# A decoder kernel on one core: the widest projection built anew with fp16 halves, its stores not waited for at its end, and one layer's queries and keys kept in SBUF

## The chip, the cores and the metric

The kernel runs on one core of a Trainium2 chip. The metric is the device time of one execution in microseconds (us). Three executions of the kernel before gave a median of 3291.48 us. The core's engines are TensorE (PE in the profile; PEld is its weight load), VectorE (DVE), ScalarE (ACT), GpSimd (POOL) and SyncE (SP), which here only issues DMAs. Each runs its own instructions in order and waits for others by semaphores.

## The reference

A decoder of four layers on x (2 x 1024 tokens of 256 numbers) and a context. Each layer is self-attention, cross-attention and a feed-forward part, each with a residual and a normalisation. Three places matter here.

Layer 0's feed-forward part sends each token to 4 of 32 experts; its end is

```
y = sum over the 4 chosen experts j of weight[t, j] * expert_out[slot[t, j]]
x = layernorm(x + y + shared)
```

Layer 1's self-attention has 16 query heads and 4 key/value heads of 64 numbers with a rotary embedding:

```
q = x @ Wq (256 -> 1024);  k = x @ Wk (256 -> 256);  v = x @ Wv (256 -> 256)
rope(a): (a1, a2) -> (a1 * cos - a2 * sin, a1 * sin + a2 * cos)
o = causal softmax(rope(q) rope(k)^T / 8) v;   x = layernorm(x + o @ Wo (1024 -> 256))
```

Layer 2's self-attention has one head of 256 numbers:

```
q, k, v = x @ Wq, x @ Wk, x @ Wv (256 -> 256 each);  o = causal softmax(q k^T / 16) v
```

## The kernel before, in words

The stages run one after another; a `Phase` holds a stage's tiles and semaphores and ends with a barrier of all engines. x lies twice in SBUF: by rows in `k.xr`, by columns in `k.xtr` (both in the tile `res`). The 2048 tokens are 16 tiles of 128, four groups (NG) of 512, two batches (B) of 1024.

**l1p**, the stage that the change rewrites, is `project_in` with `ahead=combine`. POOL gathers the four experts' rows of each tile by indirect DMA (line 2529, 64 gathers into 12 slots `yg`); VectorE adds them, weighted, onto `acc` (line 2538), adds the residual, takes the statistics (2551) and normalises (2564). TensorE turns the rows of a group into columns (2581), ScalarE copies them to `k.xtr` (2573). After two groups the projection begins, in fp32: ten jobs of 128 columns of W and 1024 tokens in each batch (line 1811, tile `res` against `l1p_w`), in pairs, "first" and "second" half of four heads, and two jobs of values. For a pair VectorE multiplies both halves by cos and sin out of PSUM into `tmp` (1886, 1887), POOL subtracts and adds into `st` (1914, 1915), ScalarE writes the fp16 upper part `his` (1830), VectorE the lower part `los = st - his` (1863), and SP stores the pair with 16 DMAs (1786) into `l_q_h`, `l_q_l`, `l_k_h`, `l_k_l` in DRAM. The additions for the third and fourth group stand between the pairs of batch 0. ScalarE doesn't write `his` before all 16 stores of the pair before have landed:

```
1829  after(act, ph.s["rstored"], 16 * 2 * job.n_dst * r)
1830  act.activation(his[:, half, :], st[:, half, :], ACT.Copy).then_inc(ph.s["hi_done"], 1)
```

At its end SP waits for all stores (1795). In batch 1 SP also loads the attention's first slot (`FirstSlot.queries`, `keys`), after batch 0's stores; POOL has filled constant rows of it (`fill`, two MEMSETs).

**l1a** is `packed_attention`. SP loads q and k of a pair of steps into a slot (`load`, lines 877 and 880), the second and third slot at the stage's start, and then moves the rows' maxima of each step (`maximum_rows`, 892). TensorE computes the maxima's products (1011) two steps ahead, then the scores (1042); the pass is shared by all engines. **l1o** is `project_columns`: o_t (1024 x 2048, fp32) against Wo in fp32 (line 1308, 8 matmuls of 256 columns a tile), then `Tail`, residual and normalisation of each group.

**l2p** is `project_in` again, in fp32, with jobs of kind "store": ScalarE copies to `st`, SP stores to DRAM (1771). **l2a** (`attention`) begins with two loads of these tensors (428, 429) and then makes its scores (460).

## Time and profile before

| | us |
|---|---|
| three executions | 3291.48, 3284.66, 3299.39 |
| the profiled execution | 3290.18 |
| its span in the profile | 3288.4 |
| PE busy | 2498.7 (76%) |
| DVE busy | 1872.2 (57%) |
| ACT busy | 1441.7 (44%) |
| POOL busy | 978.9 (30%) |

A busy share is a mean over stages that differ. The times below are counted from the start of the span. In a row of the timeline "x32" says that 32 instructions are merged, and the bracket gives the idle time before them and what ended it. An fp32 matmul leaves two records in the trace. The granted clock is a share of 2.4 GHz, and it has two levels, 1.2 and 2.4 GHz.

### The profile page before, as it was taken

Reading aid. Unit: us, or ns where it says so; the run is one execution under the profiler, and the core shown is the slowest. Engines: PE = TensorE matmul, PEld = TensorE weight load, DVE = VectorE, ACT = ScalarE, POOL = GpSimd, SP = SyncE. Lnnn points to the kernel's source line nnn. Section 1 sums busy time; section 2 is a strip of 40 time slices with the busy share of each in tenths; the row PEclk is TensorE's granted clock in tenths of the full one; section 3 lists DMA queues with packets and bytes.
Section 4 is the critical chain, followed back from the end, with each engine's and each line's share of the span. In section 5 each row is a group of like instructions: output and inputs, shape, how many; then the busy total and the mean of one; then the engine's idle time right before and its main releaser. Section 6 shows DMA issues by size and latency. Waiting matters only on the chain. (4 is left out here: it accounts for less than half of the span.)

```text
span 3288.4 us, 44258 instructions
## 1 busy us (share of the span) xinstructions
PE 2498.7 (76%) x15490; PEld 1395.0 (42%) x15490; DVE 1872.2 (57%) x5013; ACT 1441.7 (44%) x2899; POOL 978.9 (30%) x802
## 2 busy tenths in 40 slices
PE   6788885785725688888884679887776788859987
PEld 2223334564522333333362255555443333346666
DVE  6566655465748555555423558235442577656677
ACT  5334451454411256666611524214411355537876
POOL 1245561145355366666602400001101101101200
PEclk9889997897967889999986879998688799978988
DMA  3311101710555311111002210111000322114023
GB/s 111 99 36 42 42 2 36 233 50 17 156 147 90 92 54 36 45 40 36 17 14 66 34 39 1 61 52 34 14 0 27 78 28 28 16 47 122 1 78 103
DMA packets 185741, 182.87 MB, mean 56 GB/s; under 512 B 55161, under 2 KB 152187, under 8 KB 184751
## 3 DMA queue, kind: packets, MB, share of 16 engines
q1 hardware_dynamic: 176110, 167.48, 18.2%
q0 software_dynamic: 9408, 12.56, 2.6%
q8 instruction: 124, 2.03, 0.3%
q14 instruction: 99, 0.80, 0.1%
HBM read 121.81 MB, written 61.59 MB: 56 GB/s over the span
## 5 line engine op out<-in xcount | busy, mean ns | idle before, releaser
L941 POOL TENSOR_TENSOR l1a_p_lo<-res,l1a_p_hi 128x1024 f16<-128x1024 f32 x192 | 311.6, 1641 | 178.5 <-ACT res L1182 178.5
L1191 ACT ACTIVATE l0a_probs<-ps 128x1024 f32<-128x1024 f32 (+1 forms) x192 | 145.7, 810 | 178.1 <-PE ps L1045 105.7
L1191 ACT ACTIVATE l3a_probs<-ps 128x1024 f32<-128x1024 f32 (+1 forms) x192 | 146.7, 809 | 142.4 <-PE ps L1045 115.2
L1181 ACT ACTIVATE l1a_p_hi<-ps 128x1024 f16<-128x1024 f32 x192 | 157.8, 822 | 112.3 <-PE ps L1045 83.0
L1042 PE MATMUL ps<-l1a_qs,l1a_ks 128*128 128x512 f16 (+3 forms) x768 | 167.4, 332 | 32.2 <-ACT res L1182 32.2
L1213 DVE CUSTOM_DVE_ANT_0 l1a_masked<-ps,l1a_wide_mask 128x128 bf16<-128x128 f32 (+3 forms) x256 | 118.1, 490 | 103.1 <-PE ps L1011 100.7
L1011 PE MATMUL ps<-l1a_ks,l1a_qs 128*128 128x512 f16 (+3 forms) x384 | 122.0, 347 | 61.9 <-DVE l1a_nmax L1216 33.0
L966 POOL TENSOR_TENSOR l0a_both<-l0a_probs 128x768 f32<-128x768 f32 (+2 forms) x96 | 154.5, 1631 | 46.4 <-PE ps L1083 46.1
L1182 ACT ACTIVATE res<-ps 128x1024 f32<-128x1024 f32 x192 | 158.1, 824 | 0.0
L1045 PE MATMUL ps<-mask_t,ident_b 128*128 128x128 bf16 x768 | 157.9, 225 | 0.0
L1213 DVE CUSTOM_DVE_ANT_0 l0a_masked<-ps,l0a_wide_mask 128x128 bf16<-128x128 f32 (+3 forms) x256 | 116.4, 489 | 70.2 <-PE ps L1011 69.6
L1011 PE MATMUL ps<-l0a_ks,l0a_qs 102*128 102x512 f16 (+3 forms) x384 | 122.5, 356 | 28.2 <-DVE l0a_nmax L1213 19.5
L2837 PE MATMUL ps<-x_m,x_x 128*128 128x462 f16 (+1 forms) x672 | 136.0, 351 | 9.5 <-PEq L111 9.1
L1213 DVE CUSTOM_DVE_ANT_0 l3a_masked<-ps,l3a_wide_mask 128x128 bf16<-128x128 f32 (+3 forms) x256 | 113.5, 488 | 35.2 <-PE ps L1011 34.2
L1011 PE MATMUL ps<-l3a_ks,l3a_qs 126*128 126x512 f16 (+3 forms) x384 | 115.8, 360 | 10.1 <-DVE l3a_nmax L1213 6.6
L1216 DVE TENSOR_REDUCE l1a_nmax<-ps 128x1 f32<-128x512 f32 x128 | 83.8, 686 | 41.9 <-PE ps L1011 41.5
L1042 PEld LDWEIGHTS ps<-l1a_qs,l1a_ks 128*128 128x128 f16 x768 | 63.3, 99 | 94.6 <-ACT res L1182 34.4
L1042 PE MATMUL ps<-l3a_qs,l3a_ks 128*128 128x512 f16 (+3 forms) x384 | 102.5, 339 | 1.0 <-ACT l3a_probs L1191 0.7
L1811 PE MATMUL ps<-res,l1p_w 128*128 128x512 f32 x160 | 81.4, 669 | 28.1 <-DVE l1p_tmp L1887 25.9
L1011 PEld LDWEIGHTS ps<-l0a_ks,l0a_qs 102*128 102x128 f16 x384 | 32.9, 98 | 159.2 <-DVE l0a_nmax L1213 77.3
L1042 PE MATMUL ps<-l0a_qs,l0a_ks 104*128 104x512 f16 (+3 forms) x384 | 99.4, 333 | 1.1 <-ACT l0a_probs L1191 0.7
L2317 POOL MEMSET x2c_cb<- 64x154 f32 x1 | 0.2, 222 | 318.7 <-POOLq L111 318.7
(736 smaller groups left out, 6415.9 us busy)
## 6 DMA issues: line engine op xcount, KB each, us to landing
f_wf<-in_L_ffn_w_dram SPq DMA_DIRECT2D x16, 1024.0 KB
f_slots<-x0a_zeros SPq DMA_DIRECT2D x32, 256.0 KB, 3.4
f_xe<-f_slots SPq DMA_DIRECT2D x32, 256.0 KB, 3.0
f_ys<-f_y SPq DMA_DIRECT2D x32, 256.0 KB
l1a_qs<-l_q_h SPq DMA_DIRECT2D x64, 128.0 KB
d_wall<-in_L_ffn_W_dram SPq DMA_DIRECT2D x3, 2112.0 KB
l0a_qs<-l_q_h SPq DMA_DIRECT2D x32, 128.0 KB
l0a_ks<-l_k_h SPq DMA_DIRECT2D x16, 256.0 KB
```

The lines of the kernel that those rows point to most:

```text
L941: pool.tensor_tensor(ph_lo[:, n % SLOTS, :, 0:w], probs[:, n % FULL, :, 0:w], ph_hi[:, n % SLOTS, :, 0:w], ALU.subtract).then_inc(s_["low_ ...
L966: pool.tensor_tensor(both[:, heads, d:d + w], a_[:, heads, d:d + w], b_[:, heads, 0:w], ALU.add).then_inc(s_["added"], 1)
L1011: ins = pe.matmul(sa[:, col:col + f.w], qs[slot][0:stack.max_rows, 0, st.q0 // QC, f.p, q0:q0 + P], ks[slot][0:stack.max_rows, f.p if KH > ...
L1042: ins = pe.matmul(SB[x % 2][:, half, 0:w], ks[slot][0:r, p if KH > 1 else 0, d, u.key:u.key + KR], qs[slot][0:r, d, st.q0 // QC, p, u.off: ...
L1045: ins = pe.matmul(SB[x % 2][:, half, 0:P], k.ident_b[:], k.mask_t[:], start=False, stop=True)
L1181: act.activation(ph_hi[:, n % SLOTS, :, 0:w], SB[n % 2][:, :, 0:w], ACT.Exp)
L1182: act.activation(probs[:, n % FULL, :, 0:w], SB[n % 2][:, :, 0:w], ACT.Exp).then_inc(s_["exps"], 1)
L1191: act.activation(probs[0:KR, n % SLOTS, 2 * pr:2 * pr + 2, 0:w], SB[x % 2][:, :, 0:w], ACT.Exp).then_inc(s_["exps"], 1)
L1213: dve.tensor_tensor_reduce(out=masked[:, a % NSA, 0:f.w], in0=src, in1=wide_mask[:, QC - f.w:QC], scale=-1.0, scalar=3e38, op0=ALU.add, op ...
L1216: dve.tensor_reduce(high, src, AX.X, ALU.max, negate=True).then_inc(s_["maxed"], 1)
L1811: ins = pe.matmul(slot[j % 2][:, c0:c0 + w], lhsT, rhs, start=n == 0, stop=n == len(terms) - 1)
L2837: ins = pe.matmul(S[q % RING][:, 0:w], xs[x][:, d, t * P:(t + 1) * P], ms[m][:, d, i, c0:c0 + w], start=n == 0, stop=n == len(steps) - 1)
```

## The change

Three stages are changed.

l1p becomes `rotary_projection`. The residual is added to `acc` first; TensorE then sums in PSUM: an fp32 matmul of `acc` with the identity and four of the gathered rows with diagonal matrices of the experts' weights, which ScalarE writes (`summed`, `diagonals`). Statistics and normalisation read PSUM; the columns go as fp16 high and low parts into `xp`, no longer into `k.xtr`. The weights are split once into `wp`. The projection is 20 pairs of 512 tokens (`pairs`: 4 groups x 5), three fp16 products each. `tmp` and A have two buffers, `parts` four, gathers 20 slots. Each part of a pair is stored with two DMAs, the high ones by SP, the low ones by ScalarE. Tables, gathered rows, diagonals and parts lie in `l1_o_t`, the tile that the attention's output fills later. The stage doesn't wait for its last stores: their semaphores go to `early.stored`, and SP waits for them in l1a, behind `maximum_rows(0)`, before it loads the second and third slot.

l1o becomes `project_halves`: o_t and Wo are split into fp16 parts by ScalarE and VectorE, three groups deep, and each product becomes three. l2p keeps q and k in SBUF (`q_t`, `k_t`), waits for each third of the weights by itself, and l2a reads them there (`held`).

```diff
+    GS = 20
+    GATHERS = (6, 5, 5, 0, 0)
+    PB = 4
+    pairs = [(g, p) for g in range(NG) for p in range(PAIRS)]
...
@@ rotary_projection, SP
+            for n, (g, p) in enumerate(pairs):
+                if g == 2 and p == 1:
+                    all_stored(sp, 0, 2 * PAIRS)
+                    all_stored(sp, 1, 2 * PAIRS)
+                    early.queries(sp)
+                    early.keys(sp)
+                sp.wait_ge(s_["hi_done"], n + 1)
+                sp.sem_inc(s_["storing"], 1)
+                store(sp, 0, n)
...
@@ rotary_projection, POOL
+            gather(0, EACH)
+            for n, (g, p) in enumerate(pairs):
+                if g + 1 < NG:
+                    at = (g + 1) * EACH + sum(GATHERS[:p])
+                    gather(at, at + GATHERS[p])
+                pool.wait_ge(s_["mults"], n + 1)
+                if n >= 2:
+                    pool.wait_ge(s_["lo_done"], n - 1)
...
@@ rotary_projection, TensorE
+            for t in range(GT):
+                summed(t)
+            columns(0)
+            for n, (g, p) in enumerate(pairs):
+                project(n)
+                if p == 0:
+                    rows(g)
+                if g + 1 < NG:
+                    for t in {1: (0,), 2: (1, 2), 3: (3,)}.get(p, ()):
+                        summed((g + 1) * GT + t)
+                    if p == PAIRS - 1:
+                        columns(g + 1)
...
@@ rotary_projection, ScalarE
+            for n, (g, p) in enumerate(pairs):
+                if g + 1 < NG and p < 2:
+                    diagonals((g + 1) * EACH + 2 * p * K0, (g + 1) * EACH + 2 * (p + 1) * K0)
+                if p == 1:
+                    rows(g)
+                if n >= 2:
+                    act.wait_ge(s_["lo_done"], n - 1)
+                    store(act, 1, n - 2)
+                if p == PAIRS - 1 and g + 1 < NG:
+                    columns(g + 1)
+                upper(n)
+                if p == PAIRS - 2 and g + 1 < NG:
+                    roots(g + 1)
...
@@ rotary_projection, VectorE
+            for n, (g, p) in enumerate(pairs):
+                last = p == PAIRS - 1
+                if last and g + 1 < NG:
+                    normal(g + 1)
+                rotate(n)
+                if n and p:
+                    lower(n - 1)
+                if g + 1 < NG and p == PAIRS - 2:
+                    moments(g + 1, 0)
+                    moments(g + 1, 1)
+                    variances(g + 1)
+                if last and g + 1 < NG:
+                    columns(g + 1)
+                if last:
+                    lower(n)
...
@@ packed_attention
-                for tb in range(OWN, min(LOADS, TBS)):
-                    load(tb)
+                def first_loads():
+                    for sem, count in first.stored if first else ():
+                        sp.wait_ge(sem, count)
+                    for tb in range(OWN, min(LOADS, TBS)):
+                        load(tb)
...
                     maximum_rows(s)
+                    if s == 0 and late:
+                        first_loads()
...
@@ project_halves, ScalarE
+                upper(0)
+                upper_weights()
+                upper(1)
+                upper(2)
+                for g in range(NG):
+                    tail.scalar(act, g)
+                    if g == 0:
+                        upper(3)
...
@@ l2_self_attention
-        attention(k, "l2a", causal_units(D), 1, D, D, qt, kt, v_all, o_all)
+        attention(k, "l2a", causal_units(D), 1, D, D, None, None, v_all, o_all, held=(q_t, k_t))
```

How that falls out on two queues follows.

POOL in l1p, from the stage's first instruction, in the kernel before (f_ys holds the experts' rows, l1p_tmp the products with cos and sin):

```order
L2529 DMA l1p_yg<-f_ys,d_of_slot 128x256 x40
L1914 TENSOR_TENSOR l1p_st<-l1p_tmp 128x1024
L1915 TENSOR_TENSOR l1p_st<-l1p_tmp 128x1024
L2529 DMA l1p_yg<-f_ys,d_of_slot 128x256 x8
L1914 TENSOR_TENSOR l1p_st<-l1p_tmp 128x1024
L1915 TENSOR_TENSOR l1p_st<-l1p_tmp 128x1024
```

and in the changed one (the products now lie in res, gathered rows and st in l_o_t):

```order
L2044 DMA l_o_t<-f_ys,d_of_slot 128x256 x22
L2056 TENSOR_TENSOR l_o_t<-res 128x512
L2057 TENSOR_TENSOR l_o_t<-res 128x512
L2044 DMA l_o_t<-f_ys,d_of_slot 128x256 x5
L2056 TENSOR_TENSOR l_o_t<-res 128x512
L2057 TENSOR_TENSOR l_o_t<-res 128x512
L2044 DMA l_o_t<-f_ys,d_of_slot 128x256 x5
L2056 TENSOR_TENSOR l_o_t<-res 128x512
L2057 TENSOR_TENSOR l_o_t<-res 128x512
```

22 gathers stand ahead of the first rotation where 40 stood, and a group's gathers are spread over the first three pairs of the group before it.

VectorE around the end of a group's second-last pair in the changed kernel (2181 to 2196 statistics and normalisation of the next group, 2212 and 2213 products of a pair, 2220 a pair's low part, 2201 the low columns):

```order
L2220 TENSOR_TENSOR l_o_t<-l_o_t 128x1024
L2181 BN_STATS l1p_stats<-ps 128x6 x4
L2186 BN_AGGR l1p_mv<-l1p_stats 128x2 x4
L2188 TENSOR_SCALAR l1p_ve<-l1p_mv 128x4
L2192 RECIPROCAL l1p_rs<-l1p_sd 128x4
L2196 TENSOR_SCALAR res<-ps,l1p_mv,l1p_rs 128x256 x4
L2212 TENSOR_TENSOR res<-ps,l_o_t 128x512
L2213 TENSOR_TENSOR res<-ps,l_o_t 128x512
L2212 TENSOR_TENSOR res<-ps,l_o_t 128x512
L2213 TENSOR_TENSOR res<-ps,l_o_t 128x512
L2220 TENSOR_TENSOR l_o_t<-l_o_t 128x1024
L2201 TENSOR_TENSOR l1p_x<-ps,l1p_x 128x1024
```

where the kernel before had, between its pairs:

```order
L2538 SCALAR_TENSOR_TENSOR d_acc<-l1p_yg,d_weight,d_acc 128x256 x8
L2548 TENSOR_TENSOR l1p_r<-d_acc,res 128x1024
L2551 BN_STATS l1p_stats<-l1p_r 128x6 x4
L2554 BN_AGGR l1p_mv<-l1p_stats 128x2 x4
L2556 TENSOR_SCALAR l1p_ve<-l1p_mv 128x4
L1863 TENSOR_TENSOR l1p_los<-l1p_st,l1p_his 128x1024 x2
L2561 RECIPROCAL l1p_rs<-l1p_sd 128x4
```

The weighted additions are gone from VectorE; the normalisation of the next group now stands ahead of the last pair's products.

## Rows read from the trace of the kernel before

**Rows 1.** Table by stretches: busy us (instructions) of each engine, granted clock, DMA share, GB/s.
```profile
925.50:981.50 56.00, 3.91 (x16) 3.14 (x16) 25.43 (x62) 3.73 (x5) 41.68 (x40) 0.50 0.54 139
981.50:1075.00 93.50, 56.35 (x132) 28.65 (x133) 76.93 (x92) 14.53 (x17) 52.06 (x36) 0.80 0.48 85
1075.00:1146.40 71.40, 47.26 (x109) 23.08 (x107) 37.34 (x30) 12.39 (x12) 23.27 (x10) 0.85 0.40 99
...
1200.00:1300.00 100.00, 80.54 (x666) 35.93 (x664) 53.22 (x172) 63.24 (x88) 62.28 (x40) 0.98 0.17 44
```

**Rows 2.** Waits of ScalarE, 981.5 to 1146.4: waiter, releaser, us in total, times, longest.
```profile
ACT l1p_his L1830 <- DMA l_q_l<-l1p_los: 82.0, 7, 16.9
```

**Rows 3.** Timeline of l1o: start us, duration us, engine, line, operation, idle before.
```profile
1669.15 30.46 PE L1308 MATMUL ps<-l1o_w,l_o_t 128*128 128x256 f32 x128 [8.45 <-DMA l1o_w<-in_L_attn_Wo_dram]
...
1700.32 13.98 PE L1308 MATMUL ps<-l1o_w,l_o_t 128*128 128x256 f32 x64
...
1715.01 13.98 PE L1308 MATMUL ps<-l1o_w,l_o_t 128*128 128x256 f32 x64
```

**Rows 4.** Timeline around l2's projection and attention.
```profile
2089.00 0.37 SPq L1759 DMA_DIRECT2D l2p_w<-in_L_attn_Wq_dram  x1
...
2093.83 15.87 PE L1811 MATMUL ps<-res,l2p_w 128*128 128x512 f32 x32 [6.77 <-DMA l2p_w<-in_L_attn_Wv_dram]
...
2139.34 0.37 SPq L428 DMA_DIRECT2D l2a_q<-l_qt  x1
...
2152.20 1.20 PE L460 MATMUL ps<-l2a_k,l2a_q 128*128 128x128 f32 x4 [14.96 <-DMA l2a_k<-l_kt]
```

**Rows 5.** Single lines in l1p: count, ns min/median/max, first and last start.
```profile
L1863 DVE TENSOR_TENSOR l1p_los<-l1p_st,l1p_his x20: 1217/1225/2269, 1001.3 to 1136.3; 128x1024 f16<-128x1024 f32 x20
...
L1830 ACT ACTIVATE l1p_his<-l1p_st x20: 1039/1057/1058, 995.3 to 1135.0; 128x1024 f16<-128x1024 f32 x20
...
L2529 POOL DMA_INDIRECT l1p_yg<-f_ys,d_of_slot x64: 994/998/1798, 926.7 to 1043.9; - x64
...
L2538 DVE SCALAR_TENSOR_TENSOR d_acc<-l1p_yg,d_weight,d_acc x64: 472/484/5242, 933.0 to 1053.3; 128x256 f32<-128x256 f32 x64
```

**Rows 6.** Timeline of l1p up to the attention's first matmul.
```profile
950.04 0.48 DVE L2538 SCALAR_TENSOR_TENSOR d_acc<-l1p_yg,d_weight,d_acc 128x256 f32<-128x256 f32 x1 [1.48 <-DMA l1p_yg<-f_ys,d_of_slot]
950.48 1.00 POOL L2529 DMA_INDIRECT l1p_yg<-f_ys,d_of_slot  x1 [0.31 <-issue]
...
974.25 1.41 DVE L2551 BATCH_NORM_STATS2 l1p_stats<-l1p_r 128x6 f32<-128x256 f32 x4
...
976.84 1.58 DVE L2564 TENSOR_SCALAR res<-l1p_r,l1p_mv,l1p_rs 128x256 f32<-128x256 f32 x4
...
981.56 15.64 PE L1811 MATMUL ps<-res,l1p_w 128*128 128x512 f32 x32 [1.11 <-ACT res L2573]
...
1008.28 5.24 DVE L2538 SCALAR_TENSOR_TENSOR d_acc<-l1p_yg,d_weight,d_acc 128x256 f32<-128x256 f32 x1
...
1010.88 2.35 POOL L1915 TENSOR_TENSOR l1p_st<-l1p_tmp 128x1024 f32<-128x1024 f32 x1
...
1146.53 0.48 PE L1011 MATMUL ps<-l1a_ks,l1a_qs 128*128 128x128 f16 x2 [9.96 <-PEq L111]
```

**Rows 7.** Groups by shape, whole span: busy us, mean ns, idle before.
```profile
L950 POOL TENSOR_TENSOR l0a_o_raw<-l0a_o_raw,res 128x512 f32<-128x512 f32 x16 | 20.3, 1271 | 0.0
...
L1230 DVE TENSOR_TENSOR l_o_t<-ps,l1a_o_raw 128x512 f32<-128x512 f32 x32 | 22.0, 689 | 19.9 <-PE ps L1026 19.9
```

**Rows 8.** Timeline of TensorE's fp16 matmuls in another stage.
```profile
2068.81 1.46 PE L3474 MATMUL ps<-f_x,f_w 128*128 128x512 f16 x6
...
2074.43 5.41 PE L3497 MATMUL ps<-f_w,f_h 128*128 128x256 f16 x48
```

**Rows 9.** Timeline of the start of l1a.
```profile
1152.39 0.28 DVE L1224 CAST l1a_mh<-ps 8x128 f16<-8x128 f32 x1 [0.47 <-PE ps L1019]
...
1167.12 0.53 PE L1011 MATMUL ps<-l1a_ks,l1a_qs 128*128 128x128 f16 x2
```

More of the change, by code:

```diff
@@ L416, in _ @@
             def _(sp):
+                if held:
+                    return
                 with times(sp, turns) as t:
@@ L450, in scores @@
                         u = units[i]
-                        if i == 0:
+                        if i == 0 and not held:
                             pe.wait_ge(q_ld[p], 16 * t + 16)
@@ L1730, in row_parts, with project_in @@
     return parts
-def project_in(k, ph, jobs, loads, rope=None, split=False, ahead=None, early=None):
+def project_in(k, ph, jobs, loads, split=False, early=None, apart=False):
     nc = k.nc
@@ L1802, in _ @@
                     after(pe, freed[j % 2], b * (NJ // 2) + j // 2)
+                    if apart and b == 0:
+                        pe.wait_ge(w_ld[job.load], 16)
                     if job.needs:
                         pe.wait_ge(ph.s["kept"], b * len(keeps) + job.needs)
-                    if ahead and j == 0:
-                        for g in (0, 1) if b == 0 else ():
-                            ahead.columns(pe, g)
-                        pe.wait_ge(ahead.s["xts_ready"], 2 * b + 2)
                     for c0, w, terms in job.parts(b):
@@ L1812, in _ @@
                     ins.then_inc(ph.s["jobs_done"], 1)
-                    if ahead and b == 0 and j in (5, 9):
-                        ahead.columns(pe, 2 if j == 5 else 3)
         @block.scalar
         def _(act):
-            for g in (0, 1) if ahead else ():
-                ahead.roots(act, g)
-                ahead.moved(act, g)
-            act.wait_ge(ph.s["w_ld"], 16 * len(loads))
+            if not apart:
+                act.wait_ge(ph.s["w_ld"], 16 * len(loads))
             for b in range(B):
                 for j, job in enumerate(jobs):
-                    if job.kind in ("first", "second"):
-                        if job.kind == "second":
-                            for half in range(2):
-                                r = b * R + firsts.index(j - 1)
-                                act.wait_ge(ph.s["rotated"], 2 * r + half + 1)
-                                after(act, ph.s["rstored"], 16 * 2 * job.n_dst * r)
-                                act.activation(his[:, half, :], st[:, half, :], ACT.Copy).then_inc(ph.s["hi_done"], 1)
-                        if ahead and b == 0 and j in (3, 7):
-                            ahead.roots(act, 2 + j // 4)
-                        if ahead and b == 0 and j in (5, 9):
-                            ahead.moved(act, 2 + j // 8)
-                        continue
                     act.wait_ge(ph.s["jobs_done"], b * NJ + j + 1)
@@ L1970, in l0_cross_to_l1_self_attention @@
-                for dram, n, c0 in ((qt, FQ // (2 * P), 0), (kt, FK // (2 * P), FQ // P)):
-                    for g in range(n):
-                        for half, kind in enumerate(("first", "second")):
-                            jobs.append(Job(column_parts(w, xs, c0 + 2 * g + half), kind, dsts=halves(dram, g, half), n_dst=8))
-                for j in range(0, TB, 4):
-                    jobs.append(Job(row_parts(w, xs, FQ + FK, FK, j), "rows", dst=lambda b, j=j: v_all[:, ds(b * TB + j, 4), :]))
```

459 lines of the change are left out of this document (294 added, 165 removed).

## The prediction

> **What bounds the kernel now.** I read the table by stretches first, because the change touches three stretches that stand far apart and no engine is the limit of the whole. In [rows 1] the stage l1p (combination of the experts' results, then the widest projection) runs from 925.5 to 1146.4, 220.9 us. In its first 56 us VectorE is busy for 25.4 us and TensorE for 3.9 us; in the next 93.5 us VectorE is the fullest (76.9 us), in the last 71.4 us nobody is: TensorE 47.3, VectorE 37.3, POOL 23.3. So something outside the engines ends the waits. The view of waits [rows 2] names it: ScalarE stood 82.0 us, in 7 waits, before it could write his, until the stores of the previous pair had left st's halves (one counter for 16 stores of a pair, one pair of staging buffers). TensorE's next projection waits for the rotation's products on VectorE, which stand behind the low half in its queue, and the low half waits for that same ScalarE instruction. The other stretches: the projection l1o is a row of matmuls without a gap [rows 3], and l2's scores wait for the two tensors that the stage before had just written to DRAM [rows 4].
>
> **The price of each piece, from rows.** Gather on POOL: 0.998 us and 0.30 us to the next, 1.30 [rows 5, 6]. POOL's 128x512 operation: 1.27 us [rows 7], two for a rotation, 2.54. VectorE's 128x512 from PSUM: 0.69 [rows 7], four per pair, 2.76; its 128x1024 low half 1.225; ScalarE's high half 1.06 [rows 5]. TensorE in fp16: 5.41 us for 48 matmuls of 256 columns, 0.113 each, 1.46 for 6 of 512 columns with the drain, so 0.22 each [rows 8]. In fp32 64 records of 256 columns take 13.98 us and a matmul has two records: 0.44 [rows 3].
>
> **l1p after the change.** Work per group of 512 tokens: TensorE 5 pairs x 12 x 0.22 = 13.2, values 24 x 0.113 = 2.7, combination 4 x 5 x 0.44 = 8.8, transposes 1, together 25.7 us. VectorE 5 x (2.76 + 1.225) = 19.9 plus about 5.5 for statistics, normalisation and low columns. POOL 16 x 1.30 + 5 x 2.54 = 33.5. ScalarE 5 x 1.06 for high halves, 2 for columns and values, and 16 diagonals of 128x128, a size that no row here has: 0.13 each by its share of the 1.06, 1.06 as the upper bound, so 9 to 24 us, covered either way. POOL is thus the fullest in three groups of four, but a chain through all of them is longer, and I follow it.
>
> Start. The 16th gather has landed at 950.04 [rows 6], as it will: gathers set it. Now 7.3 us pass from the second group's statistics (974.25) to the first projection (981.56) [rows 6]; the addition of the residual ahead of them is moved to the stage's start, one fp32 matmul (0.9 on the slow clock) and the low columns (1.2) come in. Projection starts at 950.0 + 0.9 + 7.3 + 1.2 = 959.4 and not at 981.56, since one group and not two is waited for. Pair 0 on the slow clock: 12 x 0.43 = 5.1, last two products 1.4: 965.9. POOL: rotation 2.54, 5 gathers 6.5, rotation, 5 gathers, rotation of pair 2: T0 = 986.5.
>
> From T, the end of pair 2's rotation in a group: low half 2, delayed by one of POOL's operations, T+2.5; statistics and variance 2.0, T+4.5; root behind ScalarE's high half 3, T+5.1; reciprocal and normalisation 1.8, T+6.9 (the statistics 1.41 and the normalisation 1.58 have rows, and 4.2 us from the start of the one to the end of the other [rows 6]); products of pair 4, T+9.7; its rotation, with low half 3 between, T+13.4; 6 gathers, T+21.2; rotation, 5 gathers, rotation, 5 gathers, rotation: T+41.9. Meanwhile low columns are ready at T+13.4, the next projection gives pair 0's products by T+17.4, before POOL wants them at T+21.2. Three such points: T2 = 986.5 + 2 x 41.9 + 2.8 (the two MEMSETs for the attention's first slot) = 1073.1. In the last group nothing is gathered: pair 0's products at T2+17.4 = 1090.5, four more pairs at VectorE's 4.0 us: 1106.5; then low half 3, rotation, high and low half 4, 6.0: 1112.5. No store is waited for; one issue and the barrier, 2.3. The attention starts at 1114.8 and not at 1146.5 [rows 6]: **-31.7 us**. Stores cost nothing here: 4 DMAs a pair in place of 16, on two queues, four buffers deep; the cover is that a buffer comes round only after four pairs, 16 us or more.
>
> The disputed term is the port that VectorE and POOL share. An addition of VectorE with two operands in SBUF took 5.24 us where the median is 0.484, exactly while POOL did its two 2.35 us operations [rows 5, 6]; products from PSUM don't show this, as the 128x512 ones of l1a with POOL beside them keep 689 ns [rows 7]. The low half has two operands in SBUF. The lower bound of a meeting is 0, the upper both operations, 2.54; I take one, 1.27, because the low half becomes ready about when the first ends. The Trainium skill, page "SBUF — State Buffer", section "Who interferes with whom", has it that such a VectorE instruction and a POOL one that reads SBUF exclude each other for the whole of one instruction, so the loser would wait for one. By that rule the stretch ends at 1112.5; by the 5.24 us row, with both operations waited for at two places of three groups and once in the last, it would end 7 x 1.27 = 9 us later. The trace shows both kinds.
>
> **Start of l1a.** SP now issues 18 loads before the row maxima of step 0; after the change the maxima go first and the loads behind them. The maxima's halves are ready 6 us into the stage (1152.39), the load of the second slot is wanted at 1167.12 [rows 9], 20.6 us in. Two issues of 0.7 and nine of 0.64 from 6.2 us end at 13.4, and 3 us for landing leave 4 us of cover. The last stores are issued before the barrier, so they are done by then. I put 0; if the cover is gone, at most the second slot's 7 us.
>
> **l1o.** Now 8.45 us of wait for the weights, then 128 fp32 matmuls of two records each, 14.0 us a group and 14.7 from group to group with the transposes (1700.32 to 1715.01), the first group 30.46 - 13.98 = 16.5 on the slow clock [rows 3]. After: the weights still land at 1669.15, then two copies of 1.06 and two low halves of 1.2, offset by one: 3.5 us later. A group is 96 x 0.113 = 10.8, with transposes and their drain 12.0; the first 13.3, as the slow clock now costs 16.5 for 14.0. Group 0 is ready at 1686.0 as now (1669.15 + 16.5 = 1685.7). Then 3 x (14.7 - 12.0) = 8.1 less, of which about 1.8 goes back: ScalarE copies group 3's halves only behind the columns of group 0, VectorE waits for them before the second tail. **-6.3 us**.
>
> **l2.** The first matmul waits for its own third of the weights: now 4.8 us after the first issue, the third being issued 0.9 later [rows 4]; I take 2.1 less (0.9 to 2.8). After the projection the scores start with the stage and not after the reload: 2152.20 - 2139.34 = 12.9, of which the first matmul needs no more than 0.1. ScalarE's copy takes as long into SBUF as into st, and TensorE is unbroken there. **-14.9 us**.
>
> **Sum.** -31.7 - 6.3 - 14.9 = -52.9 on the profiled execution's own 3290.2 us (its span is 3288.4): 3237.3. It stands 1.3 us below the median of the three runs, 3291.5, so I say 3239.
>
> **Rivals.**
> (a) POOL alone sets the pace and the chain through VectorE hides: 33.5 a group. 986.5 + 2 x 33.5 + 2.8, then 17.4 + 16 + 6 + 2.3: 1098.0, 17 us less: **3222**. For it: POOL is in fact the fullest; against it: the normalisation stands in VectorE's order between pairs 3 and 4.
> (b) The chain is longer: both of POOL's operations are waited for (+9), the semaphore hops cost, and the second slot's load comes late (+7): **3255**. For it: the 5.24 us row, and 15 hops in a group that I counted at nothing.
> (c) Stores still pace it. A pair's two DMAs carry 4x32 rows of 512 halves each, a shape that no row shows. If a round of a buffer took the 16.9 us of the longest wait now, four buffers would still allow a pair every 4.2 us, so it costs 1 us here. The change would not do what it says only if a round took above 30 us; then 20 pairs at 8 us and more leave the stage as long as now: **3270**.
> (d) Slower: TensorE's clock. The granted clock is 0.50 (the 1.2 GHz level) in the stretch where TensorE has 3.9 us of work in 56, and 0.98 in the attention from 1200 on [rows 1]. If the fuller TensorE of l1p and the warmer start made the grant fall in the 514 us of l1a (1146.5 to 1660.7, where l1o's wait for its weights begins [rows 3]), that stage would stretch, as TensorE is busy there for 80.5 of 100 us. It decides from 52.9 + 16.5 = 69 us, a stretch by 13.5%, so a grant of about 0.86: **3308**. Against it: 0.98 to 1.00 is held there at 80% busy. That the clock stays at 0.50 all through l1p instead makes TensorE's part 51 us a group and ends the stage at about 1150, only 36 us more, still below now in sum.
>
> **Chances.** Forecast, 3226 to 3250: 0.48. (a) 0.20. (b) 0.22. (c) 0.05. (d) 0.05. The range reaches past (a) and past (b): 3210 is (a) less 12, for a load wait and a clock term that I may have counted too dear; 3262 is (b) and 7 for hops. (c), (d) and a few extremes lie outside. Half a per cent, 16.5 us, is about what a measurement of this kernel tells from no change. Faster 0.92, same 0.04, slower 0.04.
>
> **What would show it.** The profile after should have no DMA wait before ScalarE's high half in l1p; POOL's rotations at 1.27 us; the first fp16 projection near 959.4; groups 42 us apart on POOL; l1a's first matmul near 1115, with its first score matmuls 17 us into the stage as now; l1o's four groups 12 us apart; l2a's first matmul within 0.2 us of the stage. It is wrong where gathers stretch above 1.3 us beside VectorE's work, where TensorE's combination waits for single gathers in a way that holds the next projection up, or where l1a, whose order of loads alone changes, takes another time than its 514 us.

## The result, and the profile after

The changed kernel takes **3262.03 us** (median of five runs, 3261.13 to 3271.12) against 3291.48 (3284.66 to 3299.39) before: ratio 0.9914, 95% interval 0.9896 to 0.9933, so 29.5 us less, and 22 to 34 by the interval. The forecast was 3239 with a range of 3210 to 3262: the direction is right, the gain is little more than half of the 52.9 forecast, and the median lies at the range's upper edge, by 0.03 us outside. Run again later in four timed runs it gave 0.9903 (0.9889 to 0.9918), 3258.8 against 3293.3, which is 34.5 less.

Stages first, cut at their first loads or, for the attentions, where their first scores appear. Four windows of the kernel before, l1p, l1o, l2's attention and its output projection (from:to, length, then busy us and instructions of PE, PEld, DVE, ACT and POOL, granted clock, DMA share, GB/s):

```profile
925.97:1146.53 220.56, 107.52 (x257) 54.90 (x258) 139.71 (x184) 30.68 (x34) 117.05 (x87) 0.74 0.47 103
...
1662.37:1738.05 75.68, 62.69 (x288) 54.53 (x288) 18.94 (x64) 6.20 (x9) 0.00 (x0) 0.88 0.05 15
...
2139.34:2226.87 87.53, 72.93 (x328) 53.28 (x328) 30.05 (x56) 14.60 (x33) 0.00 (x0) 0.92 0.13 48
2226.87:2260.50 33.63, 22.74 (x128) 19.03 (x128) 18.95 (x64) 10.32 (x17) 0.00 (x0) 0.96 0.03 8
```

and six of the changed kernel, l1p, l1a, l1o, l2's projection, attention and output projection:

```profile
940.98:1146.78 205.80, 133.94 (x529) 73.04 (x530) 102.94 (x167) 52.52 (x101) 134.31 (x107) 0.79 0.42 108
1146.78:1657.80 511.02, 410.43 (x3392) 183.41 (x3392) 277.00 (x882) 321.31 (x450) 327.24 (x199) 0.97 0.15 38
1657.80:1724.56 66.76, 49.63 (x416) 42.95 (x416) 39.55 (x82) 23.46 (x27) 0.00 (x0) 0.86 0.05 17
2073.56:2122.21 48.65, 43.73 (x134) 25.61 (x135) 0.00 (x1) 13.03 (x13) 0.00 (x0) 0.94 0.05 17
2122.21:2194.92 72.71, 70.69 (x323) 51.21 (x322) 30.14 (x56) 13.87 (x33) 0.00 (x0) 1.00 0.00 1
2194.92:2231.90 36.98, 25.05 (x128) 20.84 (x128) 18.94 (x64) 10.33 (x17) 0.00 (x0) 0.87 0.03 8
```

l1p lost 14.8 us where 31.7 were forecast, l1o 8.9 (6.3 forecast), l2's three stages 13.2 (14.9), l1a 4.8 (0). With 2.0 between l1o and l2 that would be 43.7, and the two spans differ by 29.0. The rest is in the starts: l1p begins at 940.98 and not at 925.97, 15.0 us that are lost in stages whose code the change doesn't touch. So two things need explaining: l1p's missing 17 us, and those 15. The starts of l1p and of l1a in the changed kernel, with POOL's gathers that took longer than their usual 1.00 us and the VectorE work beside them (2224 adds the residual, 2228 writes the low parts of the weights; start us, duration us, engine, line, operation):

```profile
940.98 0.38 SPq L2023 DMA_DIRECT2D l1p_w<-in_L_attn_Wq_dram  x1
...
941.03 4.63 DVE L2224 TENSOR_TENSOR d_acc<-d_acc,res 128x1024 f32<-128x1024 f32 x4 [3.69 <-PEq L111]
...
941.74 1.45 POOL L2044 DMA_INDIRECT l_o_t<-f_ys,d_of_slot  x1 [5.79 <-POOLq L111]
...
943.50 1.92 POOL L2044 DMA_INDIRECT l_o_t<-f_ys,d_of_slot  x1 [0.31 <-issue]
...
949.15 3.50 DVE L2228 TENSOR_TENSOR l1p_w<-l1p_w 128x1024 f16<-128x1024 f32 x3 [3.49 <-ACT l1p_w L2154]
...
949.64 1.61 POOL L2044 DMA_INDIRECT l_o_t<-f_ys,d_of_slot  x1 [0.30 <-issue]
...
1146.78 0.48 PE L1027 MATMUL ps<-l1a_ks,l1a_qs 128*128 128x128 f16 x2 [17.33 <-PEq L111]
```

The DMA wait ahead of ScalarE's high half is gone [rows 2]. Waits in l1p after (waiter, releaser, us in total, times, longest):

```profile
ACT l_o_t L2149 <- POOL l_o_t L2057: 110.5, 20, 10.3
POOL l_o_t L2056 <- DVE res L2213: 43.2, 10, 9.4
...
DVE res L2212 <- PE ps L2098: 34.6, 11, 7.0
```

ScalarE now waits for POOL's rotations, POOL for VectorE's products, VectorE for TensorE: a ring through all four, as forecast, but longer.

### The profile page after: what moved, and what is told of

Its sections match the earlier page's. It is cut to its first block and busy times, and to the rows that moved or that the text cites. A ratio compares the mean times of both kernels' runs of the same rounds, so it can differ in the third digit from the quotient of the medians.

```text
span 3259.4 us, 45104 instructions
## 1 busy us (share of the span) xinstructions
PE 2507.8 (77%) x15890; PEld 1397.9 (43%) x15890; DVE 1855.3 (57%) x5014; ACT 1480.6 (45%) x2984; POOL 997.8 (31%) x822
## 5 line engine op out<-in xcount | busy, mean ns | idle before, releaser
L1027 PEld LDWEIGHTS ps<-l1a_ks,l1a_qs 128*128 128x128 f16 x384 | 35.5, 97 | 139.9 <-DVE l1a_nmax L1232 47.2
L3055 PEld LDWEIGHTS ps<-x_m,x_x 128*128 128x128 f16 x672 | 69.8, 104 | 59.6 <-issue 16.2
```

The costliest lines, as they stand in the source:

```text
L1027: ins = pe.matmul(sa[:, col:col + f.w], qs[slot][0:stack.max_rows, 0, st.q0 // QC, f.p, q0:q0 + P], ks[slot][0:stack.max_rows, f.p if KH > ...
L3055: ins = pe.matmul(S[q % RING][:, 0:w], xs[x][:, d, t * P:(t + 1) * P], ms[m][:, d, i, c0:c0 + w], start=n == 0, stop=n == len(steps) - 1)
```

## The experiments

### Is the later start of l1p the program's doing? The change in two parts

r1 is the kernel before, r2 the changed one, once more each. r3 has l1p's part of the change alone:

```diff
-        project_halves(k, "l1o", o_t, FQ // P, a["L1_attn_Wo"])
+        project_columns(k, "l1o", o_t, FQ // P, a["L1_attn_Wo"], None)
 (and l2_self_attention as before)
```

and r4 the new l1o and l2 on the kernel before, with its old l1p.

> The kernel before, once more. In the two traces at hand the stages ahead of l1p, whose code the change does not touch, end at 925.97 before and at 940.98 after, 15.0 us apart. Theory A: the changed program itself causes this, so l1p begins within 4 us of 926 here. Theory B: executions differ by that much among themselves, so l1p may begin anywhere from 922 to 941. Both expect l1p (its first load to the first matmul of l1a) to take 220.5 us within 1 us.

> The changed kernel, once more. Theory A (the program causes the later start): l1p begins within 4 us of 941. Theory B (executions differ): anywhere from 922 to 941. Both: l1p takes 205.8 us within 1.5, l1o's four groups and l2 as in the trace at hand; l1a 511 to 516 us, by how many short stretches at half the granted clock fall into it (four before, one after, about 1.6 us each).

> The changed kernel with the projection l1o and the stage l2 as before, so it has the change in l1p and the order of loads in l1a alone. By the stages of the two traces l1p is 14.8 us shorter. Theory A (the later start comes with this part): the time is that of before within 5 us, 3287 to 3293, and l1p begins near 941. Theory B: 3272 to 3279, and l1p begins near 926 to 930 on average.

> The kernel before with the new projection l1o and the new stage l2, and l1p as before. By the stages of the two traces l1o is 8.9 us shorter and l2 with what follows it up to the next stage 13.2 us, together 22.1. Theory A (the later start comes with l1p's part): 3266 to 3272, l1p begins near 926. If it came with this part instead (the place of tensors in DRAM, two of which are gone), 3279 to 3286 and l1p begins near 941. Theory B: 3266 to 3276.

r3 gave 3280.61 against 3296.22 (0.9956, 0.9940 to 0.9973), r4 3274.41 (0.9938, 0.9919 to 0.9957); r1 and r2 one run each, 3291.92 and 3262.92. The stages of one trace each, in us (each row below the first is the difference of two starts; x0a is the cross-attention of layer 0):

```
                        before   r1      r4     | after    r2     r3     r8
start of l1p            925.97  932.37  936.77  | 940.98  934.28 939.40 935.17
of that, stage x0a      192.31  202.04  201.22  | 198.87  201.10 202.14 199.71
l1p                     220.6   225.1   226.1   | 205.8   208.7  208.7  206.2
l1a                     515.8   510.8   513.7   | 511.0   514.4  514.3  514.4
l1o                      75.7    75.4    66.2   |  66.8    65.9   74.3   65.9
l2, three stages        171.5   171.6   158.3   | 158.3   161.2  172.2  161.4
```

The two windows of r1 that correspond, x0a and l1p:

```profile
615.20:817.24 202.04, 152.53 (x1056) 111.19 (x1056) 117.48 (x367) 97.96 (x350) 99.63 (x108) 0.85 0.27 96
932.37:1157.43 225.06, 107.50 (x256) 54.42 (x257) 140.06 (x184) 30.78 (x34) 116.40 (x87) 0.74 0.44 101
```

Theory A fell and theory B holds for r1 and r2: 932.4 is more than 4 us from 926, and 934.3 more than 4 from 941. Two of the expected starts were missed: theory B had 926 to 930 for r3, which began at 939.4, and theory A had 926 for r4, which began at 936.8. The trace that I predicted from had a stage x0a of 192.3 us that the six others of the table, of either kernel, put at 199 to 202 (and the other seven of this study at 197 to 202); that is 6.6 of the 15 us. Another 6.6 lie between x0a and l1p, 115.3 us before and 121.9 after, where the other twelve traces have 115.1 to 119.6. The l1p of the first trace was short as well, by 4.5 and 5.5 us against r1 and r4, so r1 misses what both theories expected of it (220.5 within 1), as r2's 208.7 misses 205.8 within 1.5. Executions differ by this much where neither code nor order does. l1p starts at 926 to 937 in the three traces with its old form and at 931 to 942 in the eleven with the new one, on average 4 us later; 4 us of a real effect are not excluded by three against eleven, 15 are. By the traces of both kinds l1p gains (225.1 + 226.1 + 220.6) / 3 - (205.8 + 208.7 + 208.7 + 206.2) / 4 = 223.9 - 207.3 = 16.6 us. The medians agree: 15.6 for l1p's part, 21.8 for the other, 37.4 in sum; 3280.61 is 1.6 us above theory B's 3272 to 3279, which was reckoned from a time before of 3291 and not from the 3296 that was measured beside it.

> The changed kernel again, in many runs. The two parts measured apart gave 3280.6 and 3274.4 against 3296.2, together 37.4 us less. If the parts add up, this gives 3257 to 3261 beside a before of 3296, a gain of 35 to 39 us; if not, the recorded gain of 29.5 us stands and it gives 3265 to 3268.

3258.8 against 3293.3. The time lies where the parts add up (3257 to 3261); the gain of 34.5 is just below its 35 to 39, and with an interval of 27 to 37 us it rules neither reading out. Summed over these traces, the change's own stages give 16.6 + 8.9 (l1o, 75.1 to 66.2) + 12.0 (l2, 171.8 to 159.8) = 37.5.

l1a's 4.8 us belong to no part either. Its instructions keep their distance to those of before to 0.1 us over long stretches and then step by 1.6 us where one trace has a short stretch of granted clock 0.5 (four from 1200 to 1640 before, one after). The fourteen traces bear it out, whatever their l1p: with one such stretch l1a takes 510.8 and 511.0 us, with three 513.3 to 514.4, with four 515.3 to 516.2.

### What makes l1p's groups 45 to 48 us long

POOL around the start of the second group of the changed kernel: the end of the rotation of pair 2, the rotations of pairs 3 and 4, then gathers, of which one is shown, and a group later the end of pair 2's rotation again. Between them stand VectorE's low half of pair 2, and ScalarE's high half of pair 3 and its root for the next group's normalisation.

```profile
1003.13 1.27 POOL L2057 TENSOR_TENSOR l_o_t<-res 128x512 f32<-128x512 f32 x1
...
1006.17 1.22 DVE L2220 TENSOR_TENSOR l_o_t<-l_o_t 128x1024 f16<-128x1024 f32 x1
1006.33 2.18 POOL L2056 TENSOR_TENSOR l_o_t<-res 128x512 f32<-128x512 f32 x1 [1.92 <-DVE res L2213]
...
1009.76 1.06 ACT L2149 ACTIVATE l_o_t<-l_o_t 128x1024 f16<-128x1024 f32 x1 [4.27 <-POOL l_o_t L2057]
...
1010.73 0.19 ACT L2135 ACTIVATE l1p_sd<-l1p_ve 128x4 f32<-128x4 f32 x1
...
1015.53 2.18 POOL L2056 TENSOR_TENSOR l_o_t<-res 128x512 f32<-128x512 f32 x1 [5.80 <-DVE res L2213]
...
1034.15 1.75 POOL L2044 DMA_INDIRECT l_o_t<-f_ys,d_of_slot  x1 [0.31 <-issue]
...
1050.71 1.27 POOL L2057 TENSOR_TENSOR l_o_t<-res 128x512 f32<-128x512 f32 x1
```

The rotation of pair 2 ends 63.4, 111.0 and 156.3 us into the stage (1004.4, 1052.0, 1097.2), the last rotation at 197.4 and l1a begins at 205.8. Counted from the same start the prediction had 60.5, 105.2, 147.1, 184.2 and 188.8. So it is late by 2.9 at the first group, 2.9 and 3.4 more at the next two, 4.0 more in the last, 3.8 more at the end. POOL idles 1.9 and 5.8 us ahead of the rotations of pairs 3 and 4, and only then comes to the next gathers. The 5.8 us are a chain that starts with POOL itself: its rotation of pair 3 ends at 1009.7, ScalarE writes the high half, only then the root (line 2135; the variance was ready at 1009.76, as the high half began), VectorE the reciprocal, the normalisation and the products of pair 4. Whether the root ahead of the high half shortens it was not tried. r5 leaves the chain as it is and fills those gaps with gathers:

```diff
-    GATHERS = (6, 5, 5, 0, 0)
+    AHEAD = (13, 2, 1, 4, 5, 3, 2, 2, 4, 5, 3, 2, 2, 0, 0) + (0,) * 5
...
-                if g + 1 < NG:
-                    at = (g + 1) * EACH + sum(GATHERS[:p])
-                    gather(at, at + GATHERS[p])
+                at = EACH + sum(AHEAD[:n])
+                gather(at, at + AHEAD[n])
```

> The changed kernel with POOL's gathers spread over all five pairs of a group (3, 2, 2 before pairs 0 to 2, then 4 and 5 of the group after next before pairs 3 and 4; 13 before the first rotation), where it has 6, 5, 5, 0, 0. Theory A: l1p's group of 45 to 48 us is a chain that goes through POOL's gathers, and then again through the landing of the last gather (3 us behind the rotation of pair 2, where the statistics wait for it) while POOL idles 1.9 and 5.8 us before pairs 3 and 4. Then three groups lose 6 to 9 us each and l1p takes 180 to 190 us instead of 206 to 209: 16 to 26 us faster than the changed kernel. Theory B: POOL's own work and the port set the group (16 gathers, 10 operations, contention: 37.5 us is still under 45), so at most 5 us are won. Theory C: TensorE's slow clock sets it; no gain.

3237.85 us (0.9839, 0.9826 to 0.9851), and l1p 182.2 us. The figures are theory A's: 24 us less in the stage, 21 in the median against r8. POOL's wait for the products, over the whole stage:

```profile
POOL l_o_t L2055 <- DVE res L2212: 21.3, 6, 5.8
```

21.3 us where the changed kernel has 43.2: the 22 us that POOL no longer idles are nearly all of the gain.

r9 asks which of the two effects it was, the filling or the earlier landing of a group's last gather:

```diff
-    GATHERS = (6, 5, 5, 0, 0)
+    GATHERS = (8, 8, 0, 0, 0)
```

> The changed kernel with POOL's 16 gathers of a group as 8, 8, 0, 0, 0 before the five rotations instead of 6, 5, 5, 0, 0. POOL does the same work up to pair 2's rotation and idles as long before pairs 3 and 4, but the last gather of a group is issued one rotation and 5 gathers earlier, so that its landing and the combination of the last tile no longer follow the rotation of pair 2. Theory A (late landing is one of two separate causes): 2 to 3 us less in each of three groups, l1p 197 to 201 us against 206 to 209. Theory B (only POOL's idle time counts): l1p 205 to 209. In the spread version both causes are gone, 24 us.

3259.59 us (0.9902), l1p 202.8, POOL's wait:

```profile
POOL l_o_t L2056 <- DVE res L2213: 43.1, 10, 6.6
```

43.1 us, as much as before the edit. l1p's 202.8 lies between the two theories' ranges, 3 us shorter than in the changed kernel, as much as it differs between traces of one kernel. The 3 us are in the lengths of the 64 gathers, 69.7 us in sum against 72.4, since fewer of them meet a low half of VectorE (next section). None of it is in the groups' distance: the ends of the rotations of pair 2 stand 48.5 and 45.7 us apart, where they stood 47.6 and 45.3. The median didn't move (0.9902 against 0.9903), so theory A fell: the late landing is seen in the trace of the changed kernel (TensorE's last combination waits for it), but an earlier one gains nothing by itself. The test isn't a clean one: POOL did not idle as long as before ahead of pair 3's rotation, as was assumed, but 3.6 us instead of 1.9 to 2.4. A group is POOL's work plus what it idles: the longest idle, ahead of the stage's first rotation, fell from 9.4 to 6.6 us, and the groups idled that much longer.

### The port that VectorE and POOL share

In the rows above the first rotation operation takes 2.18 us instead of 1.26 at 1006.33 and 1015.53, and the gather at 1034.15 1.75 instead of 1.00. Each starts within a low half of VectorE, which itself keeps its 1.22 us. The addition of the residual, which has two operands in SBUF as well, stretched the stage's first two gathers to 1.45 and 1.92, and the low parts of the weights two later ones to 1.61 and 1.97. In these meetings POOL's operation starts second, and POOL waits, not VectorE. r10, on r5:

```diff
-                dve.tensor_tensor(parts[1][:, n % PB, :, :], st[:, n % 2, :, :], parts[0][:, n % PB, :, :], ALU.subtract).then_inc(...)
+                for half in range(2):
+                    ins = dve.tensor_tensor(parts[1][:, n % PB, half, :], st[:, n % 2, half, :], parts[0][:, n % PB, half, :], ALU.subtract)
+                ins.then_inc(s_["lo_done"], 1)
```

> The spread version with VectorE's low half as two instructions of 512 columns instead of one of 1024. In the traces a POOL rotation operation takes 2.18 us instead of 1.27 and a gather 1.74 instead of 1.00 where it starts within a low half of 1.22 us. Theory A (each holds the shared port for the whole of one instruction): the held-up POOL operations shrink to about 1.6 us and gathers to 1.3, l1p 2 to 4 us shorter than the spread version's 182. Theory B (the port stays with VectorE as long as it has work): 2.18 and 1.74 stay, l1p 182 or up to 1 us more for 20 more instructions.

3234.0 us (0.9829, 0.9807 to 0.9851), l1p 179.7. Some of POOL's rows that were held up in r10, and VectorE's two halves of a pair in the last group:

```profile
1004.39 1.62 POOL L2055 TENSOR_TENSOR l_o_t<-res 128x512 f32<-128x512 f32 x1
...
1075.53 2.24 POOL L2055 TENSOR_TENSOR l_o_t<-res 128x512 f32<-128x512 f32 x1 [5.80 <-DVE res L2212]
...
1089.01 2.36 DVE L2220 TENSOR_TENSOR l_o_t<-l_o_t 128x512 f16<-128x512 f32 x2
...
1089.17 1.65 POOL L2055 TENSOR_TENSOR l_o_t<-res 128x512 f32<-128x512 f32 x1 [2.72 <-DVE res L2212]
```

Of nearly all that are held up the same can be said: they now take 1.6 to 1.7 us, as theory A had it: half a low half, half the delay. One stays at 2.24. The stage is 2.5 us shorter in one trace and the median 3.9, neither more than a hint; what the rows show is the delay itself. They show too why so little comes of it. 15 of the 40 rotation operations are now held up where r5 has 9, so that in sum they take 57.4 us and not 57.8; only the gathers fall, from 73.2 to 68.5. In the last group VectorE's second half starts behind POOL's operation and waits in its turn (2.36 us for the two), and there the pairs come 4.6 to 4.7 us apart where r5 has 3.5 to 4.8. Of the 5 us that POOL works less, 4 come back as idle time ahead of its rotations (26.5 us against 22.4). The Trainium skill, page "SBUF — State Buffer", section "Who interferes with whom", says that such a pair excludes each other for a whole instruction; these rows agree for the rotations, with 0.92 us of delay by an instruction of 1.22. The same section infers that the generation of a gather's descriptors is not held up by a tensor_tensor of VectorE, since it needs the shared pair's write side and the tensor_tensor takes only the read side; the gathers of 1.75 and 1.92 us say otherwise, and their delay shrinks with the low half as the rotations' does (1.2 to 1.4 us in r10). In r5 a VectorE instruction is the loser too: the variance, 128x4 elements and 0.17 us elsewhere, started within a gather (1036.96 to 1037.96) and took 3.10 us, until both operations of the rotation behind it had ended:

```profile
1037.41 3.10 DVE L2187 TENSOR_SCALAR l1p_ve<-l1p_mv 128x4 f32<-128x4 f32 x1
...
1037.98 1.27 POOL L2055 TENSOR_TENSOR l_o_t<-res 128x512 f32<-128x512 f32 x1
1039.20 1.26 POOL L2056 TENSOR_TENSOR l_o_t<-res 128x512 f32<-128x512 f32 x1
```

### The stores at the end

The last issues of l1p in the changed kernel, on two queues:

```profile
1139.60 1.31 SPq L2012 DMA_DIRECT2D l_k_h<-l_o_t  x2
1140.80 4.17 ACTq L2012 DMA_DIRECT2D l_k_l<-l_o_t  x2
```

and a window of it (columns as in the tables by stretches):

```profile
1140.00:1145.00 5.00, 0.00 (x0) 0.00 (x0) 0.77 (x1) 0.00 (x0) 0.00 (x0) 0.50 0.27 95
```

The last two issues on ScalarE's queue take 4.17 us together, where an issue has a median of 0.526. In the window VectorE alone has 0.77 us of work left, and the DMAs move 95 GB/s. A pair's four stores of 128 KB need 512 KB / 95 GB/s = 5.5 us at that rate, and the last pairs come 4.5 us apart. The 16 DMA engines are busy for 0.27 of this window; what holds the rate at 95 GB/s there is open.

r6 waits for all stores within the stage, r7 gives the last two pairs' low stores to SP:

```diff
@@ r6
                 store(sp, 0, n)
+            all_stored(sp, 0, len(pairs))
+            all_stored(sp, 1, len(pairs))
 (and early.stored stays empty, so that l1a's loads go first again)
@@ r7
+            for n in (len(pairs) - 2, len(pairs) - 1):
+                sp.wait_ge(s_["lo_done"], n + 1)
+                store(sp, 1, n)
 (and the same loop is gone from ScalarE)
```

> The changed kernel with the wait for all stores put back at the end of l1p, and the first loads of l1a ahead of the first row maxima again. Theory A: the stores flow at 10.6 ns a packet of 1 KB on both queues together and a backlog stands at the end (two issues of ScalarE's queue take 1.6 and 2.6 us where 0.53 is usual), so the wait costs what is left of it: 3 to 8 us slower than the changed kernel. Theory B, as predicted: the last stores land 2 to 3 us after their issue; 2 to 3 us slower, and the order of the loads is worth nothing.

> The changed kernel with the last two pairs' low-half stores issued by SP instead of ScalarE. Theory A (the rate of all stores together limits): SP's issues at the end take 1.5 to 3 us in place of ScalarE's, l1a's first matmul still comes 8 us after POOL's last rotation, and the time is the same within 2 us. Theory B (ScalarE's queue is slow to issue): all issues take 0.5 us, the end comes 3 to 4 us earlier.

r6: 3271.2 us (0.9936, 0.9921 to 0.9950), l1p 213.9 us. r7: 3256.74 (0.9903, 0.9882 to 0.9924), 2 us from r8's 3258.8, l1p 208.7. The end in r6 and SP's queue in r7:

```profile
1136.70 2.61 ACTq L2011 DMA_DIRECT2D l_k_l<-l_o_t  x1
...
1150.23 0.48 PE L1027 MATMUL ps<-l1a_ks,l1a_qs 128*128 128x128 f16 x2 [26.44 <-PEq L111]
```

```profile
1132.04 3.68 SPq L2012 DMA_DIRECT2D l_q_l<-l_o_t  x2
1135.76 3.00 SPq L2012 DMA_DIRECT2D l_k_l<-l_o_t  x2
```

In r6 the last store is issued at 1136.7 to 1139.3, and the attention starts 10.9 us later, 17.5 us behind POOL's last rotation where the changed kernel has 8.4 to 9.3. Theory B fell for both. Theory A has the mechanism, not all of the numbers: moved to the other queue, the issues are as slow there (3.68 and 3.00 us for two), but on one queue they stand behind each other, and l1a begins 11.2 us behind the last rotation where 8 were expected. The Trainium skill, page "DMA: Bandwidth & Descriptors", section "Issuing engines are not separate DMA queues", says that an engine's own queue saves only its issuing time; r7 agrees. It is the stores together that are behind, and not waiting for them is worth about 8 us of l1p's gain (213.9 against 206.2 in r8, with 3 us between traces of one kernel). The median differs by 12.4, more than theory A's 3 to 8; r6's runs spread over 3262 to 3275, so the stage's figure is the better one.

The DMA queues from 985 to 1146 (packets, MB, share of 16 engines), of before and of the changed kernel:

```profile
q1 hardware_dynamic: 8784, 11.68, 27.2%
```

```profile
q1 hardware_dynamic: 6112, 6.16, 11.8%
q10 hardware_dynamic: 4799, 4.77, 9.2%
```

A packet was 1.33 KB on average and is now 1.0, since a row of a group of 512 tokens has 1 KB where one of half the tokens had 2. That the smaller packets make the rate was not tried alone.

### Two further versions

r11, on r5, puts VectorE's low half two pairs behind the products; r12, on r10, starts with 9 gathers ahead of the first rotation and shifts the others.

```diff
@@ r11
-                if n and p:
-                    lower(n - 1)
+                if n >= 2:
+                    lower(n - 2)
@@ r12
-    AHEAD = (13, 2, 1, 4, 5, 3, 2, 2, 4, 5, 3, 2, 2, 0, 0)
+    AHEAD = (9, 4, 3, 5, 5, 3, 2, 1, 5, 4, 3, 2, 2, 0, 0)
```

> The spread version with each low half two pairs behind the products instead of one. In the last group a pair takes 4.5 us: products, POOL's rotation, high half, low half in one ring. Theory A: VectorE alone then sets the pair (2.45 + 1.22 = 3.7 us) and POOL's rotation starts behind the low half, not beside it: last group 3 to 5 us shorter, the other groups up to 1 us, l1p 177 to 180. Theory B: the stores' rate (512 packets of 10.6 ns, 5.4 us a pair) takes over at the end and the issues before l1a take longer, so that l1p stays at 181 to 183.

> The version with split low halves, with the gathers as 9, 4, 3, 5, 5 in the first group and 3, 2, 1, 5, 4 and 3, 2, 2 in the next two, since 13 gathers before the first rotation end 4 us after its products are ready, and POOL still idles 1 to 3 us before pair 3's rotation. Theory A (POOL's filling is what counts): 2 to 4 us less in l1p than 179.7, and 3229 to 3233. Theory B (the chain through VectorE and TensorE now sets the group): l1p 179 to 181 and no change against 3234.

r11: 3248.45 us (0.9862, 0.9840 to 0.9883), l1p 192.6 (10 us more than r5). Neither theory had that. The last four pairs did come 3.7 to 4.7 us apart in place of 4.5, but six low stores were then issued late and together:

```profile
1109.43 2.21 ACTq L2012 DMA_DIRECT2D l_q_l<-l_o_t  x2
...
1113.04 4.59 ACTq L2012 DMA_DIRECT2D l_q_l<-l_o_t  x2
1117.67 6.27 ACTq L2012 DMA_DIRECT2D l_k_l<-l_o_t  x2
```

Here six issues take 13.1 us, and the attention begins 12.7 us behind the last rotation: 4.6 us of the 10 against r5's 8.1. The other 5.8 were lost ahead of the last rotation, and POOL's rows show where:

```profile
1093.10 1.27 POOL L2055 TENSOR_TENSOR l_o_t<-res 128x512 f32<-128x512 f32 x1 [8.81 <-DVE l_o_t L2219]
```

POOL's rotation may not overwrite a buffer of st before VectorE has written the low half of two pairs ago, and r11 puts just this low half behind the products. So POOL now waits for the low half: 31.6 of its 37.6 us of idle time ahead of rotations, which in r5 are 22.4. The hold-ups at the port are nearly gone (one of 40 rotation operations is held up, 51.7 us in sum against 57.8), and the stage is longer all the same.

r12: 3239.53 us (0.9834, 0.9810 to 0.9859), l1p 184.8. Theory A fell. Theory B's time is met, its 179 to 181 for l1p is not: POOL idles 30.1 us ahead of its rotations. By their intervals r5, r10 and r12 (0.9839, 0.9829, 0.9834) can't be told apart.

## Why the prediction was right and where it failed

**Right.** The direction, and two of the sum's three terms within 3 us. The DMA wait is gone, 30 of POOL's 40 rotation operations take their 1.26 us, the first rotation ends 44.0 us into the stage where 42.5 were forecast (965.9 + 2.54 from 925.97), and l1a's first scores come 17.2 us into its stage, as before. The nearest rival is (b), a longer chain, at 3255. Its reasons were not the ones: it had VectorE wait for POOL, where POOL waits for VectorE, and the second slot's load come late, where the scores start as before. l2's projection starts 2.69 us into its stage where it was 4.83 [rows 4], 2.1 less as forecast, and its scores follow at once. The rows:

```profile
2076.25 15.40 PE L1896 MATMUL ps<-res,l2p_w 128*128 128x512 f32 x32 [4.80 <-DMA l2p_w<-in_L_attn_Wq_dram]
...
2121.43 0.68 PE L465 MATMUL ps<-l_k_t,l_q_t 128*128 128x128 f32 x4 [2.23 <-ACTq L512]
```

The attention's stage is 14.8 us shorter, more than the 12.8. Of this 3.3 went back in the output projection: its granted clock is 0.87 where it was 0.96, and the first 16 of its 256-column matmuls took 5.41 us in r2 against 3.72 in r1. Before, the attention's window had the lower clock (0.92, now 1.00), part of it in the wait for the reload, where it cost nothing. l1o gained 8.4 to 9.5 and not 6.3:

```profile
1667.23 23.89 PE L1377 MATMUL ps<-l1o_w,l1o_o 128*128 128x256 f16 x192 [11.30 <-DVE l1o_w L1419]
...
1691.82 10.64 PE L1377 MATMUL ps<-l1o_w,l1o_o 128*128 128x256 f16 x96
...
1704.70 10.64 PE L1377 MATMUL ps<-l1o_w,l1o_o 128*128 128x256 f16 x96
```

Its first matmul comes 9.4 us into the stage (10.3 forecast), and from the third group's to the fourth's is 12.9 us where 12.0 were forecast; of the 1.8 us "given back" at most the 1.3 appear that TensorE waits for VectorE's normalisation ahead of the fourth group.

**Failed.** The term that was mis-sized is l1p's: 31.7 us forecast, 14.8 measured against the trace I had, 16.6 over several. The stage was to last 188.8 us and lasts 205.8. Four steps of its sum failed:

1. "The 16th gather has landed at 950.04, as it will: gathers set it." The work that the change puts at the stage's start, the addition of the residual and the low parts of the weights, held up four gathers by 3.0 us in all (1.45 and 1.92, 1.61 and 1.97 us for 1.00). A step that I costed on its own engine cost another engine its time. The steps up to the first rotation gave 1.4 of it back, and two more gathers, beside low halves, took 1.6 (1.86 and 1.74 us). It is 2.9 at the first group.
2. "T+41.9" for a group: 2.9 and 3.4 more. I charged the shared port to VectorE, one POOL operation of 1.27 for a meeting. In the trace POOL loses: 0.92 in each of two rotations and 0.75 in two or three gathers of a group, 3.3 to 4.1 us, on the engine that I had found the fullest. So much is in the rows; that a group gets shorter by what the hold-ups lose is not shown, since in r10 most and in r11 all of it came back as idle time.
3. The last group, 4.0 more. Pair 0's rotation ended 23.2 us behind T2 and not 19.9: its projection took 4.24 us, at a granted clock of 0.63, where I used the 2.7 of the fast one, and the low columns ahead of it were 1.3 us late, since the last combination waited for its gathers:

```profile
1102.03 1.48 PE L2076 MATMUL ps<-l_o_t 128*128 128x256 f32 x4 [1.53 <-DMA l_o_t<-f_ys,d_of_slot]
```

4. "Stores cost nothing here: the cover is that a buffer comes round only after four pairs." 3.8 more at the end. I priced a store by its round trip and its issue, never by the rate of all of them. Rival (c) asked for a round above 30 us and was the wrong test; it takes no more than the last group's pairs, at 5.5 us of stores each, coming every 4.5 us. r6 and r7 bear this step out.

These are 17 us. What the prediction named as signs of being wrong came true in part: 11 of the 64 gathers took 1.45 us and more, and a combination waited for gathers. Apart from these four steps stands what the prediction took as given, the schedule: step 2's 41.9 already held POOL's idle time before pairs 3 and 4, and r5 shows that 24 us lay in it.

The other miss, the 15 us ahead of l1p, was in the comparison of two single executions: the one before was the earliest of fourteen at l1p (its x0a was 5 to 10 us shorter than in the thirteen others), the one after was the second latest. Against it stand l1a's 4.8, of the same kind, and 2.0 from l1o to l2. Sum: -52.9 + 17.0 + 15.0 - 4.8 - 2.6 (l1o) - 2.0 + 1.7 (l2) = -28.6, where the two spans differ by 29.0. The medians need no such account: they compare several executions on either side, and their 29.5, and 34.5 the second time, against the 52.5 of the forecast leave 18 to 23 us, of which l1p is 17. Rivals (a) and (d) did not occur: POOL alone never set the pace, and the granted clock in l1a is 0.97.

## What to carry to other kernels

Where two engines hold each other up, sum the fullest engine's operations in their held-up length, and check which of the two waits by a row with both in it. Don't expect the whole of it back: where the engine also waits in a ring, what it works less it may idle more, as in r10 and r11. Fill its waits first, as r5 did. A queue of stores has a rate as well as a latency: bytes of the last few steps over the measured GB/s, against the time in which they come. And before one trace's stages are the yardstick, ask for a second trace: here stages without any change differ by 5 to 10 us, up to a third of the gain.

## What was not expected of the hardware

- An issue of a store takes 0.53 us as a median and 1.5 to 3 us at the end of the stage, where many earlier stores are still under way (r6); the queue, ScalarE's or SP's, makes no difference (r7).
- A meeting of VectorE and POOL on two operands in SBUF costs POOL, where it starts second, 0.92 us by a VectorE instruction of 1.22, about 0.4 by one of half the length; where the second half starts behind POOL's operation, VectorE waits. A tiny VectorE instruction that started within a gather waited 2.9 us, past both operations of POOL's next rotation.
- Within one stage the stretches of half clock fall in other places from one execution to the next, with the order changed or not. In l1a each of the 3.4 us stretches costs 1.6 us: 511 us with one, 514 with three, 516 with four.
